# Pre-norm attention and table-weight FFN on one core: the look-up's leaves in a rotating set of buffers, and the first token group's preparation placed inside the second batch's mix and fold

## The reference

```python
x = x + attn(layernorm(x), Wq, Wk, Wv, Wo)
#   q, k, v = x @ Wq, x @ Wk, x @ Wv
#   scores = (q^T k) / sqrt(16)      512 x 512 per batch, over channels
#   softmax over the last axis; out = (weights @ v^T)^T @ Wo
x = x + ffn(layernorm(x), lut, gate_idx, up_idx, down_idx)
#   w = lut[idx], lut has 16 entries
#   gate, up: 1376 x 512; down: 512 x 1376
#   h = silu(x @ gate^T) * (x @ up^T); y = h @ down^T
```

## Time and profile before

| | us |
|---|---|
| median of 3 runs (lowest, highest) | 1169.69 (1167.72, 1170.33) |
| the profiled execution | 1168.55 |
| its span, first to last instruction | 1166.7 |
| PE busy | 1045.0 (90%) |
| DVE busy | 498.8 (43%) |
| ACT busy | 402.5 (35%) |
| POOL busy | 302.7 (26%) |
| mean granted TensorE clock | 0.953 |

### The profile page before, as it was taken

The page is one execution under the profiler, slowest core; times in us unless marked ns, Lnnn a source line. Parts: engine busy times, 40 slices in busy tenths (PEclk is TensorE's granted clock), DMA queues, the critical chain, the costliest instruction groups (busy, mean ns, idle before and its releaser), DMA issues.

```text
span 1166.7 us, 13045 instructions
## 1 busy us (share of the span) xinstructions
PE 1045.0 (90%) x4744; PEld 854.8 (73%) x4744; DVE 498.8 (43%) x972; ACT 402.5 (35%) x654; POOL 302.7 (26%) x278
## 2 busy tenths in 40 slices
PE   3978988737677779999999999999999999999997
PEld 3867866525555567888888888888878888888885
DVE  5796889987898532222221312221231223222001
ACT  4876575655555322112212121221212122122111
POOL 4734234455656201111111111121111111111111
PEclk9998989859888888999999999999999999999999
DMA  7851011210000103001000300010030001000000
GB/s 264 264 189 42 22 44 44 107 50 10 10 7 8 36 1 144 1 1 39 35 1 1 145 1 1 1 72 1 1 134 12 1 1 72 1 1 37 1 1 37
DMA packets 25708, 53.47 MB, mean 46 GB/s; under 512 B 2912, under 2 KB 16496, under 8 KB 21296
## 3 DMA queue, kind: packets, MB, share of 16 engines
q1 hardware_dynamic: 20864, 50.47, 11.9%
q10 hardware_dynamic: 4752, 2.16, 0.7%
q0 software_dynamic: 32, 0.01, 0.1%
HBM read 37.89 MB, written 14.75 MB: 45 GB/s over the span
## 4 chain that ended last, share of the span: by engine, by line
PE 61%; issue 1%; DVE 0%; POOLq 0%; POOL 0%; ACT 0%; DVEq 0%
PE bank L840 41%; PE bank L991 18%; PE bank L854 1%; PE bank L887 1%; DVE x1b L1269 0%; POOLq L60 0%; POOL h_lo L599 0%; DVE h_full L1248 0%; ACT h_hi L815 0%; DVEq L60 0%
## 5 line engine op out<-in xcount | busy, mean ns | idle before, releaser
L840 PE MATMUL bank<-x2t_hi,w_hi 128*128 128x512 f32 (+1 forms) x704 | 277.9, 395 | 11.9 <-DVE x2t_lo L1150 7.2
L840 PE MATMUL bank<-x2t_hi,w_lo 128*128 128x512 f32 (+1 forms) x704 | 276.3, 392 | 0.0
L840 PE MATMUL bank<-x2t_lo,w_hi 128*128 128x512 f32 (+1 forms) x704 | 275.6, 392 | 0.0
L1248 DVE TENSOR_TENSOR h_full<-bank,h_gate 128x512 f32<-128x512 f32 (+1 forms) x88 | 60.7, 690 | 472.6 <-PE bank L840 472.5
L599 POOL TENSOR_TENSOR h_lo<-h_full,h_hi 128x512 fp32r<-128x512 f32 (+1 forms) x77 | 99.4, 1290 | 591.7 <-ACT h_hi L815 591.7
L991 PE MATMUL bank<-w_hi,h_hi 128*128 128x512 f32 (+1 forms) x352 | 148.1, 421 | 35.4 <-DVE h_lo L1077 35.4
L840 PEld LDWEIGHTS bank<-x2t_hi,w_hi 128*128 128x128 f32 (+1 forms) x704 | 132.3, 188 | 45.2 <-issue 9.8
L806 ACT ACTIVATE h_gate<-bank 128x512 f32<-128x512 f32 (+1 forms) x88 | 52.4, 596 | 312.2 <-PE bank L840 312.2
L840 PEld LDWEIGHTS bank<-x2t_lo,w_hi 128*128 128x128 f32 (+1 forms) x704 | 131.8, 187 | 30.3
L840 PEld LDWEIGHTS bank<-x2t_hi,w_lo 128*128 128x128 f32 (+1 forms) x704 | 132.2, 188 | 29.7
L991 PE MATMUL bank<-w_lo,h_hi 128*128 128x512 f32 (+1 forms) x352 | 143.5, 408 | 0.0
(11 more groups left out here) (120 smaller groups left out, 1283.0 us busy)
## 6 DMA issues: line engine op xcount, KB each, us to landing
xg<-in_L_attn_x SPq DMA_DIRECT2D x8, 1024.0 KB, 5.7
x1a<-in_L_attn_x SPq DMA_DIRECT2D x4, 1024.0 KB, 4.8
x1b<-in_L_attn_x SPq DMA_DIRECT2D x4, 1024.0 KB, 4.8
out_dram<-x1a SPq DMA_DIRECT2D x4, 1024.0 KB, 3.9
out_dram<-x1b SPq DMA_DIRECT2D x4, 1024.0 KB, 3.9
m_hi<-m_scratch SPq DMA_DIRECT2D x3, 1024.0 KB, 6.4
m_lo<-m_scratch SPq DMA_DIRECT2D x3, 1024.0 KB, 9.7
idx_raw<-in_L_ffn_gate_idx SPq DMA_DIRECT2D x10, 256.0 KB, 5.5
```

The source lines that it names most:

```text
L840: last = pe.matmul(out_, a, b, start=(i == 0 and j == 0), stop=(i == len(terms) - 1 and j == 2))
L1248: dve.tensor_tensor(h_full[0:n, :], bank[5][0:n, :], h_gate[0:n, :], ALU.mult).then_inc(h_done, 1)
```

## The change

- A tile takes 10 looks in place of 11. Merges come in another order; POOL makes three leaves per tile (1, 4, 7), ACT five (0, 3, 2, 5, 6). Leaves 1 and 5 change their buffers every tile (`tile_of`), and each leaf is issued as soon as the merge that frees its buffer is done. The wait of `find_high` for `leaf_made` is gone.
- The items run MIX 0, TURN_V, FOLD 0, MIX 1, FOLD 1. Items of MIX 1 and FOLD 1 all use banks 0 to 3, so their products wait for the take four items back.
- The first group's steps go from FOLD 1 to MIX 0 (normalise), FOLD 0 (first `turn`), MIX 1 (`turn`, `attend`) and FOLD 1 (second normalise). `x1a` is loaded before the last three Wv parts. FOLD 1 writes to `mat_x[1]`; addresses of `wa`, `wb`, `x1a` and of chunks 4 to 7 move, and with them the tiles at which `weight_high` waits (12, 15, 21).
- The eight looks behind each step of FOLD 1 go; 140 of 330 looks stand ahead of the first FFN group.
- In the Gram stage the index tiles are shifted by one step within each four.

```diff
-        w_at = [12 * c + (8 if c >= 8 else 0) for c in range(C)]
+        w_at = [12 * c + (8 if c >= 4 else 0) for c in range(C)]
-        x1 = [at("x1a", 96, [P, T, D], F32), at("x1b", 188, [P, T, D], F32)]
+        x1 = [at("x1a", 48, [P, T, D], F32), at("x1b", 188, [P, T, D], F32)]
...
-                  (TURN_V, 0), (MIX, 0), (MIX, 1), (FOLD, 0), (FOLD, 1)]
+                  (MIX, 0), (TURN_V, 0), (FOLD, 0), (MIX, 1), (FOLD, 1)]
...
-            return bank[4 * (n // K % 2) + n % K]
+            q = n // K
+            return bank[4 * (q % 2 if q < number[(MIX, 1)] else 0) + n % K]
...
-        LEAVES = [2, 3, 7, 6]
-        POOL_LEAVES = [0, 1, 5, 4]
-        LEAVES_NEXT = {4: [0], 5: [2, 3], 6: [1, 5], 8: [4]}
-        LEAVES_SAME = {0: [7], 1: [6]}
-        tile_of_leaf = {1: 0, 2: 1, 3: 2, 4: 3, 5: 4, 6: 0, 7: 2}
+        LEAVES = [0, 3, 2, 5, 6]
+        POOL_LEAVES = [1, 4, 7]
+        LEAVES_NEXT = {4: [1], 5: [0], 6: [3], 7: [2], 8: [5]}
+        LEAVES_SAME = {0: [4], 1: [6], 2: [7]}
...
+        def tile_of(u, j):
+
+            one, five = (0, 4) if u % 2 == 0 else (4, 0)
+            return picked[u % 2] if j == 0 else part[{1: one, 2: 1, 3: 2, 4: 3, 5: five, 6: one, 7: 2}[j]]
...
             if u and j in (1, 2, 3, 5):
-                eng.wait_ge(merged, merge_count(u - 1, {1: M_WX, 2: M_RY, 3: M_XZ, 5: M_WV}[j]))
+                eng.wait_ge(merged, merge_count(u - 1, {1: M_45, 2: M_RY, 3: M_67, 5: M_WX}[j]))
             if u and j == 4:
                 eng.wait_ge(picked_done, u)
             if j in (6, 7):
-                eng.wait_ge(merged, merge_count(u, {6: M_RX, 7: M_YZ}[j]))
+                eng.wait_ge(merged, merge_count(u, {6: M_01, 7: M_23}[j]))
...
+            group, m = groups[n // K], n % K
+            if group == (MIX, 0):
+                timeline.append(("first", ("ln1", m)))
+            if group == (FOLD, 0) and m == 1:
+                timeline.append(("first", ("turn", 0)))
+            if group == (MIX, 1):
+                timeline += [("first", ("turn", m + 1))] if m + 1 < T else []
+                timeline.append(("first", ("attend", m)))
+            if group == (FOLD, 1) and m == 0:
+                timeline += [("first", "stats2"), ("rstd", NG)]
+            if group == (FOLD, 1) and m == 1:
+                timeline.append(("first", "shift2"))
+            if group == (FOLD, 1) and m in (1, 2):
+                timeline += [("first", ("ln2", 2 * m - 2)), ("first", ("ln2", 2 * m - 1))]
+            look(LOOKS_TAKE if n < 2 * K else LOOKS_SCORE if is_score(n) else LOOKS_CHAIN, room(n))
         timeline.append(("first", "x2"))
...
-                    pe.wait_ge(product_lo, n - 2 * K + 1)
+                    pe.wait_ge(product_lo, n - (2 if n // K < number[(MIX, 1)] else 1) * K + 1)
...
+                if u == 12:
+                    act.wait_ge(product_done, K * (number[(MIX, 0)] + 1))
                 if u == 15:
-                    act.wait_ge(product_done, K * (number[(MIX, 0)] + 1))
-                if u == 18:
                     act.wait_ge(product_done, K * (number[(FOLD, 0)] + 1))
-                if u == 24:
-                    act.wait_ge(product_done, LAST_ITEM)
-                if u == 30:
+                if u == 21:
                     act.wait_ge(m_stored, 16 * 2 * B)
...
                 for u in range(U):
+                    r, one, y, z, w, five = (tile_of(u, j) for j in (0, 1, 2, 3, 4, 5))
+                    dve.wait_ge(bits_found, 3 * u + 1)
+                    dve.wait_ge(leaf_made, leaf_count(u, 0))
+                    dve.wait_ge(pool_leaf_made, pool_leaf_count(u, 1))
+                    merge(0, r, one).then_inc(merged, 1)
+                    yield
+                    dve.wait_ge(leaf_made, leaf_count(u, 2))
                     merge(0, y, z).then_inc(merged, 1)
                     yield
+                    if u + 1 < U:
+                        find_high(u + 1)
+                    if u:
+                        dve.wait_ge(picked_done, u)
+                    find_bit(u, 1)
+                    find_bit(u, 2)
                     yield
+                    dve.wait_ge(leaf_made, leaf_count(u, 5))
                     dve.wait_ge(pool_leaf_made, pool_leaf_count(u, 4))
+                    merge(0, w, five).then_inc(merged, 1)
                     yield
                     if u:
                         weight_low(u - 1)
                     yield
                     dve.wait_ge(leaf_made, leaf_count(u, 6))
+                    dve.wait_ge(pool_leaf_made, pool_leaf_count(u, 7))
+                    merge(0, one, z).then_inc(merged, 1)
                     yield
+                    dve.wait_ge(bits_found, 3 * u + 3)
+                    dve.wait_ge(merged, merge_count(u, M_23))
+                    merge(1, r, y).then_inc(merged, 1)
                     yield
+                    dve.wait_ge(merged, merge_count(u, M_67))
+                    merge(1, w, one).then_inc(merged, 1)
+                    yield
+                    if u + 1 < U:
+                        find_bit(u + 1, 0)
                     yield
                     dve.wait_ge(merged, merge_count(u, M_WX))
                     merge(2, r, w).then_inc(picked_done, 1)
```

More of the change, by code:

```diff
@@ L235, in is_score @@
             return groups[n // K][0] == SCORE
[L243 to L254 removed]
+        OPS = 10
+        LEAVES = [0, 3, 2, 5, 6]
+        POOL_LEAVES = [1, 4, 7]
+        LEAVES_NEXT = {4: [1], 5: [0], 6: [3], 7: [2], 8: [5]}
+        LEAVES_SAME = {0: [4], 1: [6], 2: [7]}
+        M_01, M_23, M_45, M_67, M_RY, M_WX = range(6)
         MERGES = 6
@@ L264, in pool_leaf_count @@
             return len(POOL_LEAVES) * u + POOL_LEAVES.index(j) + 1
+        def tile_of(u, j):
+            one, five = (0, 4) if u % 2 == 0 else (4, 0)
+            return picked[u % 2] if j == 0 else part[{1: one, 2: 1, 3: 2, 4: 3, 5: five, 6: one, 7: 2}[j]]
         def leaves_at(k, mine):
[L270 to L275, removed]
+            u, p = divmod(k, OPS)
+            first = [(0, 0), (0, 1), (0, 3), (0, 2), (0, 5)] if k == 0 else []
+            both = first + [(u, j) for j in LEAVES_SAME.get(p, [])] + [(u + 1, j) for j in LEAVES_NEXT.get(p, [])]
             return [(v, j) for v, j in both if j in mine and v < U]
@@ L286, in make_leaf @@
             if j in (6, 7):
-                eng.wait_ge(merged, merge_count(u, {6: M_RX, 7: M_YZ}[j]))
+                eng.wait_ge(merged, merge_count(u, {6: M_01, 7: M_23}[j]))
             if j == 0 and u >= 2:
                 eng.wait_ge(w_lo_done, u - 1)
-            tile = part[tile_of_leaf[j]] if j else picked[u % 2]
-            return tile[:], high_bit[u % 2][:], lut_step[:, j:j + 1], lut[:, j:j + 1]
+            return tile_of(u, j)[:], high_bit[u % 2][:], lut_step[:, j:j + 1], lut[:, j:j + 1]
         timeline = []
@@ L318, in room @@
         def room(n):
-            return 15 if n < K * (number[(MIX, 0)] + 1) else 18 if n < K * (number[(FOLD, 0)] + 1) else 24
-        idx_per_tile = [1 + (i % 4 == 3) if i < T * GB else (i >= T * GB + 4) + (i == T * NG - 1) for i in range(T * NG)]
+            return 12 if n < K * (number[(MIX, 0)] + 1) else 15 if n < K * (number[(FOLD, 0)] + 1) else 21
+        idx_per_tile = [(0, 1, 2, 2)[i % 4] if i < T * GB else (i >= T * GB + 4) + (i == T * NG - 1) for i in range(T * NG)]
         assert sum(idx_per_tile) == U
@@ L679, in turn_first, with normalise @@
                 b = Block(0, 0)
[L680 to L686, removed]
-                    x2_high(b)
+                if step == "x2":
+                    x2_high(b)
+                elif step in ("stats2", "shift2"):
+                    return
+                elif step[0] == "ln1":
+                    if step[1] == 0:
+                        for i in range(4):
+                            act.wait_ge(idx_stored[i], 16 * ((U - 1 - i) // 4 + 1))
+                    normalise(b, xn_first, 0, [step[1]])
+                elif step[0] == "ln2":
+                    normalise(b, xn_first, 1, [step[1]])
                 elif step[0] == "turn":
                     x_high(b, step[1])
-            def normalise(b, into, second):
+            def normalise(b, into, second, tiles=range(T)):
                 scale, bias = rstd[second], shift[second]
@@ L699, in normalise @@
                     act.wait_ge(ln1_stats, b.n - 1)
-                for t in range(T):
+                for t in tiles:
                     act.activation(into[:, t, :], x1[b.parity][:, t, :], ACT.Identity, bias=bias[:, t:t + 1],
@@ L845, in turn_x @@
                 if b.first and t == 0:
-                    pe.wait_ge(product_lo, K * (number[(FOLD, 0)] + 1))
+                    pe.wait_ge(product_lo, K * (number[(TURN_V, 0)] + 1))
                 elif t == 0:
@@ L1084, in look_up @@
             def look_up():
-                x, y, z, w, v = part
                 find_high(0)
-                for bit in range(3):
-                    find_bit(0, bit)
+                find_bit(0, 0)
```

(13 more changed lines are left out.)

37 lines of the change are left out of this document (7 added, 30 removed).

## The result

The changed kernel takes 1174.91 us (median of 10, 1172.09 to 1178.60) against 1169.90 of the kernel before (median of 10). The ratio is 1.0046, 95% interval 1.0032 to 1.0059: slower by 5 us, where I forecast 8 us faster. The profiled execution spans 1173.5 us (1166.7 before).

What follows compares the result with a forecast made beforehand. DVE was taken to bound the kernel up to about 390 us, PE behind it. The looks' end, 243.9 + 3.1 + 19 x 7.38 - 0.5 = 386.7 for 394.5, gains 7.8 us: 1162 us from 1169.69, range 1150 to 1176.

Steps and rivals of the forecast that it cites:

- Term 1: Tiles inside the FFN: 7.38 us each on DVE in place of 8.20, with POOL's three leaves at 0.45 each.
- Rival 1: POOL leaves in the first FFN group shut DVE out for their whole 0.77 us: slower, 1180 us; chance 0.16.
- rival 2: Inside the FFN POOL's leaf still comes late and DVE waits 0.3 us more per tile: no change, 1169.6; chance 0.17.
- rival 3: A POOL leaf in the FFN costs only 0.225 us, as between 178 and 242 us: much faster, 1149; chance 0.17.
- Term 2: Up to the first take behind SCORE: 2.5 us later, between 0 and +5, at 171.4 us in place of 168.92.
- Term 3: From that take to the first FFN group: items of 2.45 us on DVE, FFN start at 243.9 for 258.8, 14.9 earlier.
- The sum: Last `h_lo` of the looks at 386.7 us in place of 394.5: gain 7.8 us, kernel time 1161.9.

Runs made afterwards that it cites:

- e1: The changed kernel with every leaf of the look-up two looks later (lag 2 in place of none): 1170.54 us, ratio 1.0023.
- e5: The kernel before with the new look-up and a lag of two looks, attention as before: 1159.72 us, ratio 0.9919.
- e2: The kernel before with the new look-up alone, no lag, attention as before: 1170.14 us, ratio 1.0006.
- e8: The changed kernel with a lag of one look in place of none: 1167.71 us, ratio 0.9984.
- e11: The kernel before with the new look-up and a lag of one look, attention as before: 1158.17 us, ratio 0.9906.
- e9: e8 with five looks behind each item of MIX 1 in place of three: 1165.77 us, ratio 0.9968.
- e10: e8 with eight looks behind each item of FOLD 1 and 24 behind the last, 184 looks ahead of the FFN: 1165.98 us, ratio 0.9971.
- e6: e1 with four looks per item in place of three: 1166.67 us, ratio 0.9977.

## Why the prediction was wrong

**Term 1 was right in kind and a little low in gain.** A tile inside the FFN takes 7.12 us; I had 7.38. From 7.12, less 5.46 of its own work and 15 h operations at 0.60 over 16.1 tiles (0.56), remain 1.10 for three leaves: 0.37 each, for which I took 0.45. Rival 1 (0.77 a leaf) and rival 2 (a late leaf; idle 2.1 us in 16 tiles) are refuted; rival 3's 0.225 is not reached either. The stretch has moved: much of it lies on `w_lo`, 903 ns long for 690, rather than on merges on `part`, 797 for 872, for which I had written over 850.

**Term 2 failed**: "I take +2.5, between 0 and +5". The take behind SCORE is at 178.10, 9.2 later than the 168.92 of the earlier trace rows. The new look-up with the old lag of 2 has it at 176.59 (e1) and, with the old attention, at 176.57 (e5); without a lag the old attention has it at 178.29 (e2). Measured from the removed lag of 2, then, 7.6 of the 9.2 come with the new look-up itself, 1.5 with the missing lag, and nothing with the attention's part. With a lag of 1 the take is earlier, 174.61 (e8) and 172.86 with the old attention (e11); measured from there the look-up's part is 3.9 and the missing lag's 3.5 to 5.4. Three executions with the same order up to here (e8, e9, e10) lie up to 1.0 apart, so the last microsecond says little. I had taken 2.8 off the load for cheaper leaves. That saving is there: the 45 merges between 90 us and this take are 33.0 us long, the 39 of the kernel before 30.9, so 0.06 less each, 2.6 in all. But the takes wait 12.3 us for ACT in that stretch where they waited 8.7, and 11.7 even with the old lag and attention (e5). ACT's fifth leaf, which I had priced at nothing by the idle time of the earlier trace rows, is the likely reason; no run has the new look-up with ACT's old share.

**Term 3 failed at its first line**, "an item 2.45". From the first take of MIX 0 (178.10) to the last of TURN_V (199.82) are seven items at 3.10: DVE waits for ACT at nearly every take. With a lag of 1 the same seven take 2.70 (e8). The FFN started at 259.65, the end of the `x2t_lo`, for the 243.9 of the forecast: 6.7 of the 15.7 from term 2, 9.0 from here, 4.5 of them in these seven items and 2.5 in FOLD 1, where each take waits 0.9 to 1.1 us for ACT. The waits that I had worked out from PE's side are there in like size: 4.6 at FOLD 0 for 3.4, 3.9 for ACT's leaf at the start of the FFN for 3.1. In MIX 1 they are 0.6, 1.2 and 0.5 at `xt_lo` for 2.6, 2.3 and 1.7, but 0.8, 1.4 and 1.0 more stand at the takes.

**The sum.** 15.7 later at the start of the FFN and 2.0 won inside it (140.8 for 142.8) put the last `h_lo` at 400.45, where I had 386.7 and the kernel before 394.52. That is 5.9 later; the span grew by 6.8.

What I did not do was to ask, of a leaf "issued as soon as its buffer is free", what stands behind it on ACT. I noted 25.6 us of ACT's idle time ahead of leaves and read it as room. It was time in which ACT was held by a semaphore, and whatever stood behind the leaf with it: ahead of the FFN, that is the takes. The removed line `LAG = 2` was in neither my quotation of the change nor a term. None of the three rivals held it either; the first only names "a like loss from the preparation", with no mechanism.

The lag is not all of it. With a lag of 1 the change takes 1167.7 (e8), so the missing lag is 7.2 of the 13.0 us between the forecast of 1161.9 and the 1174.9 measured. The other 5.8 remain: the FFN still starts 7.0 later than I had worked out, which I put down to the new look-up's load in term 2 and to PE's wait for the last `wb_lo` (16.2 us in e8) in term 3. Two slips in the prediction changed little: the 0.225 per leaf of term 2 and rival 3 still holds the 0.15 per tile that it says it takes out (0.19 without it), and the last line of the chances has those of rivals 1 and 2 exchanged.

**Why 5 us and not more.** The look-up with its lag gives 9.4 us (e5), with a lag of 1 11.5. Leaving the lag out takes all of that back where the attention is old (e2 against e5, 10.4), and 4.4 (2.7 by the ratios) where it is new. The attention's part costs 14.3 beside the old look-up, 10.8 at lag 2 and 9.5 at lag 1. I had seen its sign wrongly too: the FFN starts earlier, but each tile fewer ahead of it has to be made inside it. Between e1 and e5 4.4 tiles ahead cost 19.7 us, 4.5 each, where inside the FFN they cost 7.2. But these two differ in the attention as well. With the new attention on both sides (e8 and e10) the same 4.4 tiles cost 6.1 each. So it is in the old order that looks find waits to fill. In the new one only those behind MIX 1 do (e9: 0.8 tile moved the start by 2.4 us); behind every item (e6) or in FOLD 1 (e10) they pay nearly their full price, and giving back their number gave back 1.7 us of 9.5.

## What to carry to other kernels

Where two engines feed each other through in-order queues, an instruction placed at the very step that frees its operand makes its engine wait for the other, and all that is queued behind waits too; one step later costs nothing and was worth 7 to 12 us here. An idle time in the profile is room only if nothing that others need stands behind the waiting instruction. And moving a preparation to where it "fits" must be priced with what it displaced: here the looks that stood beside it cost some 4.5 us a tile by e1 and e5, and 6.1 in most places of the new order or some 7 inside the FFN.

## What the runs showed of the hardware

DVE and POOL, both reading SBUF, hold each other up also where DVE's instruction is a plain `tensor_tensor`. With DVE hardly idle, a `w_lo` beside a leaf took 1.08 us for 0.69, and POOL's leaves, 0.77 alone, came in groups of three that took 4.68 and 5.19 us. A pair of bit operations, which read one tile only, took 0.79 there for 0.34 (271.47):

```profile
336.69 1.08 DVE L1072 TENSOR_TENSOR w_lo<-picked,w_hi 128x512 fp32r<-128x512 f32 x1
344.05 1.08 DVE L1072 TENSOR_TENSOR w_lo<-picked,w_hi 128x512 fp32r<-128x512 f32 x1
335.36 0.79 DVE L1063 TENSOR_SCALAR bit_mask<-idx_in 128x256 int16<-128x256 int16 x2
271.47 0.34 DVE L1063 TENSOR_SCALAR bit_mask<-idx_in 128x256 int16<-128x256 int16 x2
334.28 5.19 POOL L607 TENSOR_SCALAR part<-high_bit,lut_step,lut 128x512 f32<-128x512 uint8 x3 [2.83 <-DVE picked L1056]
341.63 4.68 POOL L607 TENSOR_SCALAR part<-high_bit,lut_step,lut 128x512 f32<-128x512 uint8 x3 [2.16 <-DVE picked L1056]
```

The Trainium skill, "SBUF — State Buffer", section "Who interferes with whom", states that a DVE instruction with two SBUF inputs and a GpSimd instruction that reads SBUF exclude each other, and the `w_lo` rows agree. What it cost DVE is less than the leaf's own length, by the estimate of term 1: 0.37 us per leaf for 0.77. POOL bears the greater part, as far as the lengths tell: three leaves that alone would be 2.31 us are 4.68 and 5.19.
